# Attention with merged value products, one work bank, and results copied out of PSUM by ScalarE

## What is computed

```python
q, k = _rmsnorm(q, q_rms_w), _rmsnorm(k, k_rms_w)
gate = softplus(einsum('bthd,hd->bht', k, u_n) / sqrt(D))
bias = -dist * omega_eff[head] * gate[key]            # causal, -inf above
scores = einsum('bihd,bjhd->bhij', q, k) * scale + bias
y = einsum('bhij,bjhd->bihd', softmax(scores), v)
x = layernorm(x + y @ Wproj)
h = gelu(gelu((silu(x w1) * (x w2)) h1) h2)            # each times a scale
out = layernorm(x + h w3)
```

## Time and profile before

| | us |
|---|---|
| median of 3 runs (lowest, highest) | 3362.25 (3357.18, 3363.28) |
| the profiled execution, own time | 3363.94 |
| its span, first to last instruction | 3362.1 |
| PE busy | 3158.6 |
| DVE, ACT, POOL busy | 1671.5, 1792.8, 1491.0 |
| mean granted TensorE clock | 0.975 of full speed |

### The profile page before, as it was taken

How to read it: one execution, slowest core, us unless ns; L and a number is a source line. 1 busy time by engine, 2 the same in 40 slices (tenths; PEclk the granted TensorE clock), 3 DMA queues, 4 the chain that set the end, 5 groups by cost and what they waited for, 6 DMA issues and landing times. The chain is left out here.

```text
span 3362.1 us, 45968 instructions
## 1 busy us (share of the span) xinstructions
PE 3158.6 (94%) x15472; PEld 2462.0 (73%) x15472; DVE 1671.5 (50%) x3928; ACT 1792.8 (53%) x3057; POOL 1491.0 (44%) x1306
## 2 busy tenths in 40 slices
PE   3899999999999999999999999989999999999998
PEld 3667767667667677676676776678888888788887
DVE  6566566565565655665655656442222322232322
ACT  2477677676666766776766767742222222322222
POOL 4476676666665766766666666611111110000000
PEclk8899999999999999999999999989999999999999
DMA  2332332422432313324224225232222223111110
GB/s 74 69 86 47 84 72 47 93 62 60 95 71 67 88 44 85 68 50 93 62 60 95 62 58 147 60 120 87 86 88 86 86 85 116 65 47 67 47 67 19
DMA packets 196523, 249.12 MB, mean 74 GB/s; under 512 B 67264, under 2 KB 95040, under 8 KB 196160
## 3 DMA queue, kind: packets, MB, share of 16 engines
q1 hardware_dynamic: 196288, 246.19, 28.5%
HBM read 84.86 MB, written 43.52 MB: 38 GB/s over the span
## 5 line engine op out<-in xcount | busy, mean ns | idle before, releaser
L457 POOL TENSOR_TENSOR e_lo<-e_all,e_hi 128x512 fp32r<-128x512 f32 (+1 forms) x832 | 1034.1, 1251 | 661.4 <-ACT e_all L723 588.0
L723 ACT ACTIVATE e_all<-ps_s,bias 128x512 f32<-128x512 f32 (+3 forms) x1280 | 787.4, 622 | 168.6 <-PE ps_s L1030 82.2
L910 DVE TENSOR_REDUCE maxes<-ps_m 128x1 f32<-128x512 f32 x768 | 521.2, 686 | 374.2 <-PE ps_m L1008 371.5
L716 ACT ACTIVATE e_hi<-ps_s,bias 128x512 fp32r<-128x512 f32 (+1 forms) x832 | 559.1, 672 | 231.6 <-PE ps_s L1028 134.2
L1008 PE MATMUL ps_m<-k_ext,q_max 128*128 128x512 f32 (+3 forms) x1280 | 463.1, 383 | 55.6 <-DVE maxes L910 24.8
L1027 PE MATMUL ps_s<-q_twice,k_split 128*128 128x512 f32 (+3 forms) x1280 | 477.7, 373 | 30.2 <-ACT e_all L723 25.4
L1028 PE MATMUL ps_s<-q_ext,k_ext 128*128 128x512 f32 (+3 forms) x1280 | 471.2, 368 | 0.0
L1061 PE MATMUL ps_v<-e_lo,v_main 128*66 128x512 f32 (+1 forms) x832 | 433.6, 521 | 17.1 <-POOL e_lo L457 17.1
L1008 PEld LDWEIGHTS ps_m<-k_ext,q_max 128*128 128x128 f32 x1280 | 246.3, 193 | 205.8 <-issue 61.5
L907 DVE CUSTOM_DVE_ANT_0 ps_m<-ps_m,mask_row 128x128 f32<-128x128 f32 (+3 forms) x512 | 252.5, 496 | 284.0 <-PE ps_m L1008 283.8
L1045 PE MATMUL ps_v<-e_all,v_full 128*66 128x512 f32 (+2 forms) x896 | 324.9, 444 | 0.0
(11 more groups left out here) (245 smaller groups left out, 6127.4 us busy)
## 6 DMA issues: line engine op xcount, KB each, us to landing
q_twice<-q_max SPq DMA_DIRECT2D x256, 128.0 KB, 2.3
yt<-y_out SPq DMA_DIRECT2D x128, 130.0 KB
k_ext<-kq_hi SPq DMA_DIRECT2D x128, 128.0 KB, 2.3
q_max<-kq_hi SPq DMA_DIRECT2D x128, 128.0 KB, 2.4
k_split<-kq_hi SPq DMA_DIRECT2D x128, 128.0 KB, 2.4
k_split<-kq_lo SPq DMA_DIRECT2D x128, 128.0 KB, 2.4
q_ext<-kq_lo SPq DMA_DIRECT2D x128, 128.0 KB, 2.4
hidden<-gelu SPq DMA_DIRECT2D x64, 256.0 KB, 2.0
```

The lines of the kernel that those rows point to most:

```text
L457: on.tensor_tensor(e_lo[:, i % LO_RING, off:QB], e_all[:, u_ % E_RING, off:QB], e_hi[:, i % HI_RING, off:QB].bitcast(F32), ALU.subtract).t ...
L716: nc.scalar.activation(e_hi[:, i % HI_RING, off:QB], ps_s[u_ % 2][:, off:QB], ACT.Exp, bias=by).then_inc(hi_done, 1)
L723: nc.scalar.activation(e_all[:, u_ % E_RING, off:QB], ps_s[u_ % 2][:, off:QB], ACT.Exp, bias=by).then_inc(ex_done, 1)
L910: nc.vector.tensor_reduce(maxes[:, qt, kc:kc + 1], ps_m[m % 2][:, 0:width], AX.X, ALU.max).then_inc(mx_free, 1)
```

## The change

1. In 15 units a head (qb > 0, kt even and at most 4 qb, `merged`), `v_main` and `v_rest` lie side by side in `v_both`: 64 rounded values, a column of ones, 64 rests. One product takes its first 128 columns, which are 64 values, the ones and 63 of the 64 rests, into all 128 rows of `ps_v`. The second product of these units goes.
2. The 64th rest's share of a merged unit is summed by DVE: `e_hi` times one column of `v_both`, added up in the bank `ps_r` over the units of a block of queries; the last sum goes to `last_rest` in SBUF. PE adds it to row 63 of `ps_v` by one more product with `to_last` (128 x 64, ones in its last column), ahead of the block's last unit.
3. `ps_r` takes the place of `ps_t`, so there is one work bank, `ps_p`, and each work waits for the one just before it.
4. ACT copies `ps_v` to `y_out` instead of DVE, 128 rows for qb > 0. SP stores rows 65 to 127, the 63 sums of rests, to a new tensor.
5. `ffn_up` loads these for six of eight blocks and POOL adds them to `y_in`, which now has a place for each of the eight tiles; for block 1 that place is shared with the weights' stages, so its loads wait for those.

A few waits and places in memory follow from it (`x_rows` shares its room with `sq`, so the second sequence's rows are loaded behind the sums of pair 7).

```diff
@@ -77,6 +79,22 @@
+def merged(v):
...
+    qb, kt = UNITS[v]
+    return qb > 0 and kt <= TQ * qb and kt % 2 == 0
...
+MERGED = [v for v in range(NU) if merged(v)]
...
+def merged_before(u):
...
+    n, v = divmod(u, NU)
+    return n * len(MERGED) + sum(w < v for w in MERGED)
...
@@ -272,10 +291,11 @@
         wg = sb("wg", [P, KC, H])
-        v_main = [sb(f"v_main{i}", [P, TT, VCOLS], F32R) for i in range(2)]
-        v_rest = [sb(f"v_rest{i}", [P, TT, VCOLS], F32R) for i in range(2)]
+        v_both = [sb(f"v_both{i}", [P, TT, VB], F32R) for i in range(2)]
+        last_rest = [sb(f"last_rest{i}", [P, QB], F32R) for i in range(2)]
+        to_last = sb("to_last", [P, D], F32R)
         v_full = [sb(f"v_full{i}", [P, NQB, TQ // 2, VCOLS]) for i in range(2)]
-        x_rows = [sb(f"x_rows{i}", [P, 2, C]) for i in range(2)]
+        x_rows = kept.x_rows
         k_split = [sb(f"k_split{i}", [P, T], F32R) for i in range(2)]
...
@@ -403,16 +424,16 @@
-            return (ps_p, ps_v[0], ps_v[1], ps_t)[j % 4]
+            return (ps_p, ps_v[0], ps_v[1], ps_r)[j % 4]
...
         def work_bank(step):
-            return (ps_p, ps_t)[work_no[step] % 2]
+            return ps_p
...
-            if work_no[step] < 2:
+            if work_no[step] < 1:
                 return
-            kind, a, b = works[work_no[step] - 2]
+            kind, a, b = works[work_no[step] - 1]
             if kind == "x":
...
@@ -644,11 +680,12 @@
                             gp.wait_ge(pv_lo, count_of("PD", NU * (n - 1)))
+                            gp.wait_ge(rest_part, merged_before(NU * (n - 1)))
                     if i < 2:
-                        nc.gpsimd.tensor_tensor(v_main[s][:, rows, 0:D], v[:, rows, :], one[:, 0:1].unsqueeze(2).broadcast_to([P, HT, D]), ALU.mult).then_inc(v_hi, 1)
+                        nc.gpsimd.tensor_tensor(v_both[s][:, rows, 0:D], v[:, rows, :], one[:, 0:1].unsqueeze(2).broadcast_to([P, HT, D]), ALU.mult).then_inc(v_hi, 1)
                     elif i < 4:
                         gp.wait_ge(v_hi, 2 * n + i - 1)
-                        nc.gpsimd.tensor_tensor(v_rest[s][:, rows, 0:D], v[:, rows, :], v_main[s][:, rows, 0:D].bitcast(F32), ALU.subtract).then_inc(v_done, 1)
+                        nc.gpsimd.tensor_tensor(v_both[s][:, rows, V_REST:V_REST + D], v[:, rows, :], v_both[s][:, rows, 0:D].bitcast(F32), ALU.subtract).then_inc(v_done, 1)
                     else:
@@ -713,6 +750,8 @@
                             rest_taken(act, before)
+                            if merged(before % NU):
+                                last_rest_taken(act, before)
                         nc.scalar.activation(e_hi[:, i % HI_RING, off:QB], ps_s[u_ % 2][:, off:QB], ACT.Exp, bias=by).then_inc(hi_done, 1)
@@ -721,6 +760,15 @@
                     nc.scalar.activation(e_all[:, u_ % E_RING, off:QB], ps_s[u_ % 2][:, off:QB], ACT.Exp, bias=by).then_inc(ex_done, 1)
+                if step[0] == "take":
+                    n, qb = step[1:]
+                    grp = n * NQB + qb
+                    act.wait_ge(pv_hi, units_before(n, qb))
+                    act.wait_ge(pv_lo, count_of("PD", units_before(n, qb)))
+                    if grp >= 2:
+                        act.wait_ge(y_out_done[grp % 2], outs_before(grp))
+                    rows = slice(0, P if qb else D + 1)
+                    nc.scalar.activation(y_out[rows, grp % 2, :], ps_v[grp % 2][rows, :], ACT.Copy).then_inc(y_done, 1)
@@ -927,19 +975,31 @@
                         take_rest(dve, nc.vector, n, v)
+                    if merged(v):
+                        u_ = NU * n + v
+                        qb, kt = UNITS[v]
+                        grp = n * NQB + qb
+                        i = count_of("PD", u_)
+                        if v == MERGED[0]:
+                            dve.wait_ge(v_done, 3 * (n + 1))
+                        dve.wait_ge(hi_done, i + 1)
+                        if merged_before(u_):
+                            dve.wait_ge(rest_part, merged_before(u_))
+                        e_in = e_hi[:, i % HI_RING, :].bitcast(F32)
+                        v_last = v_both[n % 2][:, kt, V_REST + D - 1:V_REST + D].bitcast(F32)
+                        if kt == 0:
+                            nc.vector.tensor_scalar(ps_r[:], e_in, v_last, None, ALU.mult).then_inc(rest_part, 1)
+                        elif kt < TQ * qb:
+                            nc.vector.scalar_tensor_tensor(ps_r[:], e_in, v_last, ps_r[:], ALU.mult, ALU.add).then_inc(rest_part, 1)
+                        else:
+                            if grp >= 2:
+                                dve.wait_ge(pv_hi, units_before(*divmod(grp - 2, NQB)))
+                            nc.vector.scalar_tensor_tensor(last_rest[grp % 2][:], e_in, v_last, ps_r[:], ALU.mult, ALU.add).then_inc(rest_part, 1)
                 if step[0] == "first scale":
...
                     nc.vector.tensor_tensor(kept.y_first[:, c, :], kept.y_first[:, c, :], kept.r_first[:, c, :], ALU.mult).then_inc(kept.first_scaled, 1)
-                if step[0] == "take":
-                    n, qb = step[1:]
-                    grp = n * NQB + qb
-                    dve.wait_ge(pv_hi, units_before(n, qb))
-                    dve.wait_ge(pv_lo, count_of("PD", units_before(n, qb)))
-                    if grp >= 2:
-                        dve.wait_ge(y_out_done[grp % 2], 16 * (grp // 2))
-                    nc.vector.tensor_copy(y_out[0:D + 1, grp % 2, :], ps_v[grp % 2][0:D + 1, :]).then_inc(y_done, 1)
                 if step[0] == "sums out":
@@ -1042,14 +1102,22 @@
                         pe.wait_ge(ex_done, u_ + 1)
-                        nc.tensor.matmul(bank[0:VCOLS, off:QB], v_full[s][:, kt // TQ, kt % TQ - TQ // 2, :], e_all[:, u_ % E_RING, off:QB],
+                        if qb and kt == TQ * (qb + 1) - 1:
+                            last_rest_taken(pe, NU * n + max(w for w in MERGED if UNITS[w][0] == qb))
+                            nc.tensor.matmul(bank[0:D, :], to_last[:], last_rest[grp % 2][:], start=False, stop=False, skip_group_check=True)
+                        nc.tensor.matmul(bank[0:V_REST, off:QB], v_full[s][:, kt // TQ, kt % TQ - TQ // 2, 0:V_REST], e_all[:, u_ % E_RING, off:QB],
                                          start=False, stop=kt == TQ * (qb + 1) - 1, skip_group_check=True).then_inc(pv_hi, 1)
+                    elif merged(v):
+                        i = count_of("PD", u_)
+                        pe.wait_ge(hi_done, i + 1)
+                        nc.tensor.matmul(bank[:], v_both[s][:, kt, 0:P], e_hi[:, i % HI_RING, :], start=kt == 0, stop=False,
+                                         skip_group_check=True).then_inc(pv_hi, 1)
                     else:
...
                         pe.wait_ge(hi_done, i + 1)
-                        nc.tensor.matmul(bank[0:VCOLS, off:QB], v_main[s][:, kt, :], e_hi[:, i % HI_RING, off:QB], start=kt == 0, stop=False,
+                        nc.tensor.matmul(bank[0:V_REST, off:QB], v_both[s][:, kt, 0:V_REST], e_hi[:, i % HI_RING, off:QB], start=kt == 0, stop=False,
                                          skip_group_check=True)
-                        nc.tensor.matmul(bank[0:VCOLS, off:QB], v_rest[s][:, kt, :], e_hi[:, i % HI_RING, off:QB], start=False, stop=False,
+                        nc.tensor.matmul(bank[0:D, off:QB], v_both[s][:, kt, V_REST:V_REST + D], e_hi[:, i % HI_RING, off:QB], start=False, stop=False,
                                          skip_group_check=True).then_inc(pv_hi, 1)
@@ -1058,7 +1126,7 @@
                     rest_taken(pe, u_)
-                    nc.tensor.matmul(ps_v[(n * NQB + qb) % 2][0:VCOLS, off:QB], v_main[s][:, kt, :], e_lo[:, i % LO_RING, off:QB],
+                    nc.tensor.matmul(ps_v[(n * NQB + qb) % 2][0:V_REST, off:QB], v_both[s][:, kt, 0:V_REST], e_lo[:, i % LO_RING, off:QB],
                                      start=False, stop=kt - TQ * qb == TQ // 2 - 1, skip_group_check=True).then_inc(pv_lo, 1)
...
@@ -1177,7 +1246,15 @@
-            return kept.y_first[:, c, :] if i == 0 else y_in[:, (OC * (i - 1) + c) % YR, :]
+            return kept.y_first[:, c, :] if i == 0 else y_in[:, c, :]
...
+        def loaded(m):
...
+            return sum(96 if (m_ // OC + 1) % NQB else 64 for m_ in range(m % YR, m + 1, YR))
...
+        def joined(m):
...
+            return sum(1 for m_ in range(m + 1) if (m_ // OC + 1) % NQB)
@@ -1190,14 +1267,20 @@
                 sp.wait_ge(sums_out, 16)
-            if m >= YR:
-                sp.wait_ge(ylo_done, OC + m + 1 - YR)
+            if m == 0:
+                sp.wait_ge(made, 2)
+            if i == 1:
+                sp.wait_ge(wt_full, 2 * (2 * STAGES + c // 2 + 1))
+            else:
+                sp.wait_ge(ylo_done, m + 1)
             if m >= 2:
...
                 head = i * NTOK // T * H + 2 * c + j
-                sp.dma_start(y_in[j * D:(j + 1) * D, m % YR, :], yt_dram[head, 0:D, tok]).then_inc(y_load[m % YR], 16)
```

(11 more changed lines are left out.)

## The result

Changed kernel: median 3397.7 us (3392.0 to 3400.6), kernel before in the same comparison: 3359.7 us. The ratio is 1.0111, 95% interval 1.0091 to 1.0132: **1.1% slower, 38 us**, where 3385 us was forecast (23 us slower). The profiled execution took 3400.0 us (span 3398.1), the one of before 3363.9 (span 3362.1).

A forecast was written before the change was run, and what follows sets the result against it. PE was taken as the bound, except in a stretch of each pair where DVE and SP decide. -58 + 37 + 9 + 9 + 12 + 11 + 3 = +23 on 3363.9 gave 3385 us (3370 to 3402; wider range 3320 to 3432).

The forecast's parts named there:

- ScalarE +3: Attention: 128 copies of about 0.60 us each move to ScalarE, after exponentials PE is already past; +3 us (0 to 15).
- The product: Attention: 480 products of 512 columns saved, 96 added, net -89.4 us; 31.5 not gained where DVE and SP decide, so -58.
- The sums on VectorE: Attention: added sums make DVE late before the transposes, +37 us (12 to 67), and delay maxima in 1268:1286, +9 (0 to 18).
- One work bank: Projection tiles: PE waits for ACT's copy, +12 us in 15 pairs (0 to 15), +11 in the first (up to 24).
- Feed-forward 0: Feed-forward: added loads and POOL adds are covered by a layer of PE's work; 0 us, the range allowing 8.
- SyncE +9: Attention: one store of rest sums a pair lies ahead of the bias rows in SP's queue; +9 us (0 to 18).
- (1): Whole kernel: PE stays the bound throughout, DVE's gaps take all sums in; -57, 3305 us; chance 0.13.
- (2): Stretch before the transposes: DVE's lateness is at its lower end; -14, 3348 us; chance 0.17.
- (3): Attention: late DVE holds e_hi's ring of four, ACT and PE stop; +40 on the forecast, 3425 us; chance 0.20.

The follow-up runs named there:

- a4: Changed kernel without VectorE's sums of the last rest and their adding products, and with two work banks throughout: median 3298.9 us, ratio 0.9809 to before.
- b3: Kernel before with one edit, ScalarE instead of VectorE copies the results out of PSUM (128 copies): median 3339.3 us, ratio 0.9928.
- a3: Kernel before with one work bank, every work taking ps_p and ps_t left idle in attention: median 3383.6 us, ratio 1.0070.
- a2: Changed kernel without VectorE's sums of the last rest and the 96 products that add them: median 3330.4 us, ratio 0.9904 to before.
- a1: Changed kernel with two work banks, ps_p and ps_r by turns, for the first 21 works: median 3370.4 us, ratio 1.0030 to before.
- b1: Changed kernel, GpSimd scaling a block's fourth y_in tile in ffn_up only after VectorE's first two y_lo: median 3390.9 us, ratio 1.0079 to before.
- b2: Changed kernel with merged products only in query blocks 2 and 3 of a head: median 3358.2 us, ratio 0.9985 to before.

## Why the prediction came out as it did

The forecast had the sign and most of the size (3385, measured 3397.7, within its own range of 3370 to 3402), but two terms of it failed and two larger ones were off against each other. That it came within 13 us is in part luck: the terms below are off by +14, +15 and +9 one way and by -19, -4 and -2 the other. Term by term, in us of the profiled execution; the middle of the table is read from differences in the stage of pairs 2 to 16:

| step | predicted | measured | by |
|---|---|---|---|
| merged products and the rests' stores | -70 + 9 = -61 | -47 | a4 less b3 |
| copies: ScalarE +3, relief of DVE within the lateness -1.4 x 15 | -18 | -20 | b3 less before |
| one bank, 15 pairs | +12 | +8.5 (7 by a3) | a2 less a4 |
| sums, with lateness, maxima and the products that add them | 58 + 9 + 12 = +79 | +60 | changed less a2 |
| first pair | +11 | +26 | a1, a3 |
| feed-forward | 0 | +9 | b1, which took off 9.4; six stretched `y_lo` are 6.4 of it |
| sum | +23 | +36 | |

- **"The product": right in kind, too large by 14.** Its 70 splits the prediction's 58 into what is saved (480 less the 12 a pair that don't count) and what the adding products cost. The 58 took all pairs' stretches outside 1219:1268 as bounded by PE. With fewer products ACT is late there, `e_all` 50.7 us in a4 against 38.4 in b3. And the lower clock was given no term: summed over pairs 2 to 16 it stands for 34 us in the traces of before and b3, 58 in a4, 68 in the changed kernel. Products stand 0.42 us apart there (1276.19 to 1276.61) and not 0.23, so 24 us more at the lower level cost some 11. That these two make up the gap is argued, not shown: no run held the clock.
- **"The sums on VectorE": the wait was right, what it replaced was left out.** 2.5 us a pair were taken, net of the copies' relief, and the wait for `last_rest` is 2.9. But 37 + 9 for the stage, and 20 of relief beside it, came to 40 in all (60 less 20 for the products), so net to 20 and not 46. The chain that the prediction describes (gate, SP's queue, bias rows) had PE waiting behind the transposes; once PE waits for DVE ahead of them, the 16.3 us there are gone, as the waits say. The same lateness was counted as if it came on top. b2 shows which sums do it: those of block 1, and by the stretch that gets shorter the three of the odd head. Each sum costs 0.748 or 0.737 us, as the row of L896 said; TENSOR_SCALAR, taken at 0.68 between 0.37 and 0.75, costs 0.736. The Trainium skill's double rate (VectorE: DVE Perf Modes, "The perf-mode tier table") is for fp32 in SBUF; with the output in PSUM this trace shows none.
- **"ScalarE +3" was right only because of what stood beside it.** The prediction said that a gain was "excluded by nothing but the lateness of DVE, which is counted". Its relief was counted, within the +37, and nearly to the us. A reader of the sum alone would have taken the copies' edit for a small loss; by itself it is the best part of the change.
- **"One work bank", later pairs: near in size, wrong in cause.** The 12 were the wait for ACT's copy where two tiles of the projection stand together. In the traces no two tiles follow each other in pairs 2 to 16, and PE stands before none of them. The 7 us of a3 are the wait of 1.06 us a pair for the gate, less what it saves behind the transposes. The prediction named this wait, but only as one of three that end at the same late DVE; with no sums on DVE it is there too. In the changed kernel PE stands for `last_rest` instead.
- **"One work bank", first pair: the step that failed.** The working took the pitch from a row at 37.8 us, where the clock had just risen to 2.4 GHz, and added the gap to it. The bound of 24 was named ("if PE's gaps kept the clock at 1.2 GHz there"), and that is what came: a pitch of 2.89 and not 1.80. Fifteen times 2.89 less 1.07 is 27, and the first three tiles took 2 us longer than that before as well. The rows that would have decided stood in the trace of before, at 33 us, with matmuls 0.32 us apart:

```profile
33.44 0.53 PE L984 MATMUL ps_p<-w_hi,xt_lo 128*128 128x386 f32 x1
33.77 0.52 PE L984 MATMUL ps_p<-w_hi,xt_hi 128*128 128x386 f32 x1
```

  The projection begins at the low level in every kernel, so the question was not whether gaps would make the clock fall, but whether it would ever rise.
- **"Feed-forward 0": failed.** The cover named was there, since the loads were in time. What was left out is that POOL's instructions moved in time, onto the two `y_lo` at the tail that PE waits for. The trace of before holds a hint of it (five `y_lo` of 1.2 to 1.6 us away from the blocks' starts, one of 1.60 us at 2517.26, with POOL's multiplication beginning at 2517.03); the mean of a group, 753 ns, hides it.
- **SyncE +9** can't be told from the merged products in these runs; it was not tried alone.
- **Rivals.** (1) and (2) fall with the wait for `last_rest`. (3), `e_hi`'s ring stopping ACT, shows four waits for `ps_r` of at most 0.5 us, 1.9 in all; its remark on the clock, given no term, would have deserved one. The prediction read 1.00 around waits of 1.7 and 2.0 us from one pair, and that pair is no fair sample. In nine of the fifteen pairs of the kernel before the granted clock falls 9 to 19 us behind the first transposes, where these waits lie; the pair one earlier, with waits of 1.4 and 2.0, has 0.76 there (third number from the end):

```profile
1119.00:1134.00 15.00, 13.02 (x68) 8.97 (x67) 6.78 (x19) 9.63 (x17) 12.57 (x11) 1.00 0.61 137
1134.00:1141.00 7.00, 5.62 (x19) 4.00 (x20) 3.78 (x9) 4.56 (x9) 2.15 (x2) 0.76 0.59 131
```

  In the changed kernel there are again nine such falls, and eight more around the new wait of 2.9 us. The Trainium skill (TensorE: Matmul & The Clock Gate, "HAM oscillation — how this bites in real kernels") tells of idle gaps in a loop that send PE back to 1.2 GHz each time round; the traces agree in part, since it fell in most pairs but not in all.

What stays open: how much of the merged product's missing 14 us is clock and how much ACT; why PE stood at the lower clock for 37 us in b3's ffn_up and for 68 to 72 in the five other traces of the same code; and how much one instruction on DVE near the transposes costs.

## What to carry to other kernels

Look up the clock at the beginning of a phase, not in its middle: a gap of 0.6 us after each tile kept this engine at half speed through a projection of 46 us, because it came before the clock had risen. Cost each half of an edit by itself: here moving eight copies off VectorE was worth 20 us, and work put into the same stretch of VectorE's queue cost it again; a resource that is idle half the time on average is full in one stretch, and most of the price is paid by instructions in that stretch (6 us for 15 idle ones of 0.69 us by the traces, 9 to 13 by the medians). And when an edit shifts GpSimd's work in time, look for VectorE instructions with two SBUF inputs that it may now fall upon.

## What the runs showed of the hardware

- A TensorE that came to the projection at 1.2 GHz stayed there with short gaps in its work: six matmuls of 386 columns, 2.31 us, and a wait of 0.58 us, over sixteen tiles, ran 0.32 us apart throughout, in five traces; without the wait they were 0.18 us apart after 3 to 6 us, in nine. In two traces (a2, a3) the granted clock is recorded as 1.00 in this stretch although the matmuls stand 0.32 us apart: where the clock column and the distance of the matmuls differ, the distance tells.
- A VectorE TENSOR_TENSOR of 512 fp32 elements with both inputs in SBUF took 0.68 us alone and 1.75 us when it began 0.4 to 0.5 us behind a GpSimd TENSOR_TENSOR of 1.6 to 1.7 us.
- VectorE's SCALAR_TENSOR_TENSOR of 512 elements took 0.75 us with the running sum in PSUM, and 0.95 us on average with it in SBUF beside a busy GpSimd. TENSOR_SCALAR from SBUF took 0.74 us into PSUM.
